# Starting the next chunk's weights on VectorE inside the applications of the chunk ahead

## The reference

```
offsets = conv3x3(gn(x), off_w) + off_b          # 2 x 9 taps x 8 heads
aw      = sigmoid(conv3x3(gn(x), attn_w) + attn_b)
sampled = bilinear(v, base + offset)             # 4 corners, zero outside the image
head    = sum over taps of sampled * aw
x       = x + Wo @ head
x       = x + stage1(gn(x))
```

## Time and profile before

| | us |
|---|---|
| median of 3 runs | 156.76 |
| the three runs | 155.72, 156.76, 157.32 |
| the profiled execution, its own time | 156.15 |
| its span in the trace | 154.3 |
| mean granted TensorE clock over the span | 0.989 of full |

### The profile page before, as it was taken

One profiled execution on the slowest core, in us unless ns is written; L12 is line 12 of the kernel. 1 busy time (PEld: TensorE's weight loads), 2 busy tenths in 40 slices (PEclk: granted clock), 3 DMA queues, 4 the chain that ended last, 5 costly groups with the idle time before them and its releaser, 6 DMA issues.

```text
span 154.3 us, 3278 instructions
## 1 busy us (share of the span) xinstructions
PE 131.8 (85%) x1399; PEld 112.3 (73%) x1399; DVE 111.5 (72%) x197; ACT 59.0 (38%) x107; POOL 18.5 (12%) x27
## 2 busy tenths in 40 slices
PE   4976499998997999999999989998599996676780
PEld 3754499997997999998998968876376564334460
DVE  5518993395399996999969999983681878766702
ACT  3009449839905591076812180110010607003311
POOL 8931120000000000000080000000011010110100
PEclk9999879999999999999999999999999999999999
DMA  4970000049652000000000000000000000000014
GB/s 117 236 131 0 0 0 4 0 147 259 145 130 57 2 4 0 0 4 0 0 0 0 4 0 0 0 4 2 2 0 4 6 4 0 4 0 0 0 38 102
DMA packets 6675, 5.43 MB, mean 35 GB/s; under 512 B 4657, under 2 KB 5939, under 8 KB 6659
## 3 DMA queue, kind: packets, MB, share of 16 engines
q1 hardware_dynamic: 5986, 4.19, 11.8%
q10 hardware_dynamic: 672, 1.02, 2.8%
HBM read 2.79 MB, written 0.52 MB: 21 GB/s over the span
## 4 chain that ended last, share of the span: by engine, by line
PE 49%; DVE 25%; issue 8%; ACT 6%; DMA 6%; POOL 1%; SPq 1%; POOLq 0%; DVEq 0%
PE bank L980 10%; PE bank L999 9%; PE bank L1024 8%; PE bank L972 7%; DVE prod L742 6%; DMA prod<-in_w_off 6%; PE bank L933 4%; DVE part L769 3%; DVE x_t L868 3%; PE bank L1122 3%; PE bank L1155 3%; PE bank L949 2%; DVE wy L777 2%; DVE pooled L874 2%; DVE bn L594 1%
## 5 line engine op out<-in xcount | busy, mean ns | idle before, releaser
L742 DVE TENSOR_TENSOR prod<-hat,wy 128x1440 f32<-128x1440 f32 (+3 forms) x25 | 27.3, 1161 | 0.0
L769 DVE TENSOR_TENSOR part<-v,bank 128x1280 f32<-128x1280 f32 (+3 forms) x20 | 21.5, 1111 | 7.8 <-PE bank L1024 4.3
L933 PE MATMUL bank<-ones_r 128*128 128x512 f32 x83 | 23.2, 436 | 2.1 <-POOL w_pair L371 2.1
L999 PE MATMUL bank<-cst,prod 128*128 128x128 f32 (+3 forms) x189 | 22.3, 272 | 0.8 <-DVE prod L742 0.8
L999 PEld LDWEIGHTS bank<-cst,prod 128*128 128x128 f32 (+3 forms) x189 | 20.7, 132 | 1.4 <-DVE prod L742 1.0
L1024 PE MATMUL bank<-cst,part 128*128 128x128 f32 x168 | 20.9, 274 | 0.8 <-DVE part L769 0.3
L933 PEld LDWEIGHTS bank<-ones_r 128*128 128x128 f32 x83 | 17.0, 212 | 5.8 <-POOL w_pair L371 2.1
L1024 PEld LDWEIGHTS bank<-cst,part 128*128 128x128 f32 x168 | 18.3, 140 | 2.0 <-DVE part L769 1.7
L980 PE MATMUL bank<-w_cross,g_cross 128*128 128x216 f32 x144 | 19.5, 283 | 0.0
L980 PEld LDWEIGHTS bank<-w_cross,g_cross 128*128 128x128 f32 x144 | 18.2, 200 | 0.0
L972 PE MATMUL bank<-w_pair,g_pair 128*128 128x216 f32 x96 | 14.8, 294 | 3.5 <-ACT g_cross L431 3.5
(11 more groups left out here) (93 smaller groups left out, 151.6 us busy)
## 6 DMA issues: line engine op xcount, KB each, us to landing
v<-v SPq DMA_DIRECT2D x2, 480.0 KB, 6.0
v<-v SPq DMA_DIRECT2D x2, 448.0 KB, 5.6
prod<-in_w_off ACTq DMA_DIRECT2D x1, 486.0 KB, 7.1
prod<-in_w_off SPq DMA_DIRECT2D x1, 486.0 KB, 8.8
w_s<-in_w SPq DMA_DIRECT2D x4, 72.0 KB, 3.7
wc_s<-in_wc SPq DMA_DIRECT2D x2, 144.0 KB, 3.3
wp_s<-in_wp SPq DMA_DIRECT2D x4, 72.0 KB, 2.5
x_b<-in_x SPq DMA_DIRECT2D x1, 256.0 KB, 4.6
```

Source lines behind the costliest of these rows:

```text
L742: return nc.vector.tensor_tensor(prod[:, 0:K2 * CELLS * cx].rearrange("p (k q s) -> p q k s", k=K2, s=cx)[:, q0:q0 + nd], hat[:, c % 2, d0 ...
L769: nc.vector.tensor_tensor(part[:, n % PARTS, 0:nd, 0:cv].rearrange("p d (q e) -> p d q e", e=HD), moved, weights.unsqueeze(3).to_broadcast ...
L933: nc.tensor.matmul(ps.rearrange("p (a q) -> p a q", q=P), ones_r[:, :], ones_r[:, :].unsqueeze(1).to_broadcast([P, 4, P]), start=True, sto ...
L999: last = nc.tensor.matmul(out_ps[0:size, b * P:(b + 1) * P], prod[:, at:at + size], ident, start=(b == 0 and t == 0), stop=(b == n - 1 and ...
```

## The change

Row weights, edge test and first product of a chunk (together called `begin(c)` in the new code) keep their place for chunks 0 and 1. For chunks 2, 3 and 4 they are issued on DVE between the third and the fourth application of the chunk ahead (`AHEAD` = 3), behind a wait for all three `cell_ps` of that chunk, since the first product overwrites `prod`. The wait on DVE's own step counter ahead of `wy` becomes one on `hat_used`. Other products, sums and applications keep their order and shapes; no constant other than `AHEAD` is new; PE, ACT, POOL and SP are untouched.

The core of the diff (the bodies of `product` and `apply` only move out of `chunk` and are left out):

```diff
+AHEAD = 3
...
-            def chunk(c):
...
+            def row_weights(c):
+                x0, (w, cx, ck) = CHUNKS[c][0], size(c)
                 ve.wait_ge(hat_ready, c + 1)
                 ve.wait_ge(mod_ready, c + 1)
                 if c:
-                    ve.wait_ge(step, last_made[0])
-                made_wy = tick(nc.vector.tensor_tensor(
+                    ve.wait_ge(hat_used, c)
+                made_wy[c] = tick(nc.vector.tensor_tensor(
                     wy[:, :, 0:ck].rearrange("p d (k q) -> p d k q", k=K2),
...
-                ve.wait_ge(step, made_wy)
-                for i in ROWS[:-1]:
-                    product(i).then_inc(prod_ready, 1)
-                product(OWN_ROW).then_inc(hat_used, 1)
+                ve.wait_ge(step, made_wy[c])
+
+            def product(c, i):
...
+                ins.then_inc(hat_used if i == OWN_ROW else prod_ready, 1)
...
-                for i in APPLY[:-1]:
-                    apply(i)
...
+            def begin(c):
+                row_weights(c)
+                product(c, ROWS[0])
...
+            for c in range(NC):
+                if c <= 1:
+                    begin(c)
+                for i in ROWS[1:]:
+                    product(c, i)
+                if c == NC - 1:
+                    ve.wait_ge(hat_used, NC)
+                    window_test()
+                sum_own(c)
+                for i in APPLY[:AHEAD]:
+                    apply(c, i)
+                if 1 <= c < NC - 1:
+                    ve.wait_ge(cell_ps, len(GROUPS) * (c + 1))
+                    begin(c + 1)
+                for i in APPLY[AHEAD:-1]:
+                    apply(c, i)
                 if c == NC - 1:
                     ve.wait_ge(flag_ps, 1)
...
+                apply(c, APPLY[-1])
```

More of the change, by code:

```diff
@@ L730, in _ @@
                                     ALU.subtract).then_inc(w_pair_ready, 1)
-            applied = [0]
-            def chunk(c):
[L735 to L771, removed]
@@ L773, in chunk, with size @@
+            applied, made_wy, own_sum = [0], [0] * NC, [0] * NC
+            def size(c):
+                w = CHUNKS[c][1]
+                return w, w * HEADS, K2 * w * HEADS
+            def row_weights(c):
+                x0, (w, cx, ck) = CHUNKS[c][0], size(c)
                 ve.wait_ge(hat_ready, c + 1)
@@ L785, in chunk, with sum_own @@
                                                op0=ALU.add, op1=ALU.min, accum_out=vmin[:, c:c + 1])
-                ve.wait_ge(step, made_wy)
-                for i in ROWS[:-1]:
-                    product(i).then_inc(prod_ready, 1)
-                product(OWN_ROW).then_inc(hat_used, 1)
+                ve.wait_ge(step, made_wy[c])
+            def product(c, i):
+                w, cx, ck = size(c)
+                nd, d0, q0 = 2 * DX[i] + 1, WIN - DX[i], CELL0[i]
+                ins = nc.vector.tensor_tensor(
+                    prod[:, 0:K2 * CELLS * cx].rearrange("p (k q s) -> p q k s", k=K2, s=cx)[:, q0:q0 + nd],
+                    hat[:, c % 2, d0:d0 + nd, 0:ck].rearrange("p d (k s) -> p d k s", s=cx),
+                    wy[:, i:i + 1, 0:ck].rearrange("p d (k s) -> p d k s", s=cx).to_broadcast([P, nd, K2, cx]),
+                    ALU.mult)
+                ins.then_inc(hat_used if i == OWN_ROW else prod_ready, 1)
+            def sum_own(c):
+                w, cx, ck = size(c)
+                q0 = CELL0[OWN_ROW]
                 ve.wait_ge(hat_used, c + 1)
[L791 to L794, removed]
+                own_sum[c] = tick(nc.vector.tensor_reduce(
                     cell[:, :, 0:cx],
@@ L797, in chunk, with apply @@
                     ALU.add))
-                for i in APPLY[:-1]:
-                    apply(i)
+            def apply(c, i):
+                x0, (w, cx, ck) = CHUNKS[c][0], size(c)
+                nd = 2 * DX[i] + 1
+                n = applied[0]
+                applied[0] += 1
+                if c == 0:
+                    if i == WIN:
+                        ve.wait_ge(v_ready, 1)
+                    else:
+                        ve.wait_ge(v_moved[i], 16)
+                if n >= PARTS:
+                    ve.wait_ge(part_used, n - PARTS + 1)
+                if i == OWN_ROW:
+                    ve.wait_ge(step, own_sum[c])
+                    weights = cell[:, 0:nd, 0:cx]
+                else:
+                    last_group = CELL0[i] >= GROUPS[-1][0]
+                    ve.wait_ge(cell_ps, len(GROUPS) * c + (3 if last_group else 2))
+                    weights = cells_ps(c, i).rearrange("p (d q) -> p d q", d=nd)
+                xa = x0 + WIN - DX[i]
+                v0 = v[:, i, xa:xa + w, :]
+                moved = bass.AP(v0.tensor, v0.offset, [v0.ap[0], [C, nd], [HD, cx], [1, HD]])
+                nc.vector.tensor_tensor(part[:, n % PARTS, 0:nd, 0:w * C].rearrange("p d (q e) -> p d q e", e=HD),
+                                        moved, weights.unsqueeze(3).to_broadcast([P, nd, cx, HD]),
+                                        ALU.mult).then_inc(part_ready, 1)
@@ new lines, in begin, with window_test @@
+            def begin(c):
+                row_weights(c)
+                product(c, ROWS[0])
+            def window_test():
+                ve.wait_ge(far_test, NC)
+                nc.vector.tensor_scalar(vflag[:, 0, :], vmin[:, :], 0.0, None, ALU.is_le)
+                nc.vector.tensor_scalar(vflag[:, 1, :], vfar_sum[:, :], 0.0, None, ALU.is_gt).then_inc(flag_in, 1)
+            for c in range(NC):
[14 more added lines that the diff above has]
+                    apply(c, i)
```

## The result

The changed kernel takes 166.31 us (median of 6 runs, 163.65 to 167.35), the kernel before 156.94 on the same chip; ratio 1.051, 95% interval 1.041 to 1.062. Medians here are of all executions, ratios and their intervals of the fast ones alone (within 1.5% of the fastest of the same kernel): of the changed kernel 163.65, 164.14 and 165.98 us, whose mean is 164.6. Timed a second time beside its variants: 166.34 against 156.59 us, ratio 1.048 (1.041 to 1.055). The forecast of "slower" holds. The mean of 164.6 lies 1.6 us above the predicted 163.0 and in its range of 160.3 to 165.6; the median of all six lies 3.3 us above 163.0, and 0.7 above the range. The profiled execution took 163.65 us, with a span of 161.9.

A forecast was written before the change was run, and what follows sets the result against it. PE, with DVE nearly as tight, was taken as the bound, its fourth row sums made late: 2.60 + 2.51 + 1.48 = 6.6 us on 156.15 gave 162.8, and with a third of the median's 0.6 us 163.0 us; range 160.3 to 165.6.

The forecast's parts named there:

- forecast of "slower": Whole kernel: the change makes it slower, chance 0.93, against 0.03 for faster and 0.04 for the same.
- The bound and the place: PE and DVE both tight from 61 to 96 us; the held-back fourth application makes PE's queued fourth row sum wait.
- Boundaries 1/2 and 2/3: Chunk 1 to 2 and 2 to 3: PE stands 2.60 and 2.51 us ahead of the fourth row sum.
- The wait for the hats: At boundaries 1/2 and 2/3 DVE's block idles 1.3 and 1.8 us or more for ACT's hats, holding back applications.
- third rival: The hats are ready: 1.3, 0.7 and 1.5 us at the three boundaries, 3.5 in sum, 160.2 us; chance 0.05.
- Boundary 3/4: Chunk 3 to 4: fourth row sum at 96.35 in place of 94.87 us, 1.48 us later, gain included.
- Products in time, fillers covering them: Chunk 3's second product is ready 3 us before its tap sums, behind 3.7 us of filler; delays there add nothing.
- The sum: Over the three boundaries: 2.60 + 2.51 + 1.48 = 6.6 us on the profiled execution's 156.15 us, giving 162.8.
- The clock: PE's new holes of 2.5 us leave TensorE at full clock, chance 0.68; at least one fall, chance 0.2.
- signs of being wrong: Row sums of chunk 1 without a gap, block without a wait for ACT, or granted clock leaving 1.00 after a hole.
- Rival 4: TensorE's clock falls behind PE's new holes, 1.7 us each: 164.7 us for one, 166.4 for two; chance 0.2.
- Rival 1: DVE is the bound; filling its holes at boundaries 1/2 and 2/3 saves 2.8 us, 154.0 us; chance 0.03.

The follow-up runs named there:

- e4: Changed kernel with PE's order altered: two convolution columns and the fillers moved ahead of the late fourth row sums; 155.71 us, ratio 0.995 to the kernel before.
- e3: Changed kernel with ACT's last hat step cut in two, y half first, row weights waiting for that half only; 161.73 us, ratio 1.034 to before.
- e5: Changed kernel without the fillers of 16 and 10 matmuls ahead of chunk 3's and 4's tap sums; 160.41 us, ratio 1.029 to the kernel before.
- e8: Changed kernel with 9, 9 and 7 filler matmuls put ahead of the fourth row sums of chunks 1, 2 and 3; 164.01 us, ratio 1.046 to before.
- e1: The changed kernel unaltered, run and profiled again; 166.34 us against 156.59 for the kernel before, profiled execution 167.68 us.
- e7: Changed kernel with e3 and e4 together, fillers of 5 and 8 in place of 16 and 10; 155.27 us against 156.76 before, ratio 0.993.
- e10: Changed kernel, block one place later for chunks 2 and 3 only, PE's columns moved ahead of the fifth row sum, less filler; 155.21 us, ratio 0.991 to before.
- e2: Changed kernel with the block ahead at boundary 1/2 alone, chunks 3 and 4 beginning as before; 159.39 us, ratio 1.016 to the kernel before.
- e6: Kernel before the change, without the fillers of 16 and 10 matmuls; 157.64 us against 156.76, ratio 0.995 to the kernel before.

## Why the prediction was right, and where it fell short

- **The bound and the place.** Right. PE's train of row sums had no slack, and the fourth application was its next need; e4 shows it by giving PE other work there. In the kernel before that application ended at 57.31 + 1.49 = 58.80 us, 2.3 us ahead of its row sum at 61.08. The block took 3.51 us and the wait for the hats 1.3; less the 2.3, that leaves 2.5 us of lateness.
- **Boundaries 1/2 and 2/3**, forecast 2.60 and 2.51 us: the distances grew by 2.72 and 2.65 us. At boundary 1/2 the fourth row sum began at 64.67 us, its place in the train was 59.81 + 20 x 0.1094 = 62.00: 2.67 us late. Of the 0.07 over the forecast, 0.06 is the release: the row weights began 0.09 us behind the hats, where I had allowed 0.03. The idle time that the profile gives, 2.51 us, is shorter than the lateness, since it counts from the modelled end of the 20 matmuls, 59.81 + 2.35 = 62.16 us.
- **The wait for the hats** as half of it: right, 1.32 and 1.81 us of DVE's idling, 1.2 us of each hole by e3. My third rival's 0.7 us at boundary 2/3 was not reached by e3, as its y half still waited.
- **Boundary 3/4**, forecast 1.48: 1.53. The hole itself is 1.95 us and not "about 1.5": the prediction took its gain of 0.39 off the hole, but the gain lies ahead of it, in the second row sum, which came 0.33 us sooner behind the tap sums (7.15 in place of 7.48 us).
- **Products in time, fillers covering them:** right, and e5 puts a number on what they hid, 3.1 us at chunk 3.
- **The sum** of the lateness, 6.6 us: 6.90 in the trace, 6.6 in e8's one run at the clock of the best ones of before.
- **The clock** is the step that failed. "The new holes are nearer to the one that cost nothing", at 0.2 for any fall, was an argument from two stretches, and the 0.8 weight on none was wrong: e1 shows two falls of 1.6 us behind 2.5 and 2.4 us, and nine of 13 runs lie in the longer group. One of the prediction's own signs of being wrong, that the granted clock leaves 1.00 after a hole, came true in e1. Rival 4's two-fall time, 166.4 us, is within 0.1 us of the median. The price of one fall, 1.7 us forecast, measured 1.6. The forecast of 163.0 us comes near the four shortest of the 13 executions only (163.65 to 164.14).
- **Rival 1, DVE as the bound:** refuted as priced. Filling DVE's two holes left it with 7.1 us of others. Its condition, over 5 us of other work on PE, came from no row, and e4 shows that 3.65, 3.76 and 2.39 us are enough to take the holes away; the time then was 155.7 us and not 154.0, with the fillers still in PE's order. The rule in the Trainium skill, "Perfetto Trace Analysis", section Identifying Performance Opportunities, is to look for the gaps of the most-contended engine in the stretch in question. I had used it on DVE for its 16.86 of 17 us, but that is the stretch from 79 to 96 us. DVE's two gaps lie at 58.8 to 60.2 and 76.9 to 78.3 us; from 61 to 79 PE was busy for 17.83 of 18 us and DVE for 16.37, so that by occupancy the rule points at PE there. This case doesn't speak against it. With PE's order made for it (e7, e10) the early start does pay, 1.9 to 2.1 us between tap sums.

## What to carry to other kernels

Before work is put into a gap of one engine, ask of each instruction behind it when its consumer needs it, and whether that consumer has other work queued ahead: the gap here was 1.39 us, the block 3.51 us, and the application behind it was ready only 2.3 us before it was needed. A prerequisite that was met at the old place (the hats) may not be at the new one. Filler of fixed length hides an earlier start as well as a late one, so it has to be shortened or moved in the same step; and each new hole on PE should be charged with a chance of a clock fall, here 1.6 us each.

## What the runs showed of the hardware

The granted clock fell to its lower level behind PE idle stretches of 2.51 and 2.41 us in e1, of 2.51 us in e2, of 3.28 us in e6, of 1.95 us in e5 and of 1.61 us in e8, and did not behind the same 2.51, 2.41 and 1.95 us in the changed kernel's first profile. In e5 it stayed at full behind 2.51 and 2.41 us and fell behind the shorter 1.95; in the kernel before it stayed at full behind 1.79 us at the place where e8 fell behind 1.61. So the length of a single idle stretch doesn't settle it, and the same program falls in one execution and not in the next. What else decides was not found.

The fall need not come during the idling: in e1 it was there when PE resumed behind the first hole, and it came 1.4 us after PE had resumed behind the second; in e2 1.0 us after, in e8 1.3. The 1 us windows give these times to about 0.1 us.
